# Spreading the first layer's edge-group sums over 27 of the 32 FFN steps of a tile

## The reference

```python
# layer 0, h = layernorm(x)
agg = segment_sum(h[src] * w1, dst)              # 256 features an edge
deg = segment_sum(ones, dst)
x = x + concat(agg / max(deg, 1), h) @ W.T + b
# experts of 512 hidden features, relu, top 2 of 8
x = x + sum_e combine_e * (relu(layernorm(x) @ W1_e + b1_e) @ W2_e + b2_e)
# layer 1: p = relu(layernorm(x) @ Wp.T + bp), 128 features an edge
x = x + p @ W1.T + b1 + sqrt(segment_sum(w * (p*p)[src], dst)) @ W2.T + b2
# experts of 256 hidden features, gelu, top 2 of 8
```

## Time and profile before

| what | us |
|---|---|
| median of the 3 runs | 3453.04 |
| the profiled execution | 3462.63 |
| its span, first to last instruction | 3460.8 |
| PE busy | 2546.9 (74%) |
| DVE busy | 1772.4 (51%) |
| ACT busy | 1138.6 (33%) |
| POOL busy | 1687.6 (49%) |
| mean granted TensorE clock | 0.87 of full speed |

### The profile page before, as it was taken

One profiled execution on the slowest core, in us unless ns is written; L12 is line 12 of the kernel. 1 busy time (PEld: TensorE's weight loads), 2 busy tenths in 40 slices (PEclk: granted clock), 3 DMA queues, 4 the chain that ended last, 5 costly groups with the idle time before them and its releaser, 6 DMA issues.

```text
span 3460.8 us, 47385 instructions
## 1 busy us (share of the span) xinstructions
PE 2546.9 (74%) x17983; PEld 1431.0 (41%) x17983; DVE 1772.4 (51%) x4296; ACT 1138.6 (33%) x1835; POOL 1687.6 (49%) x1678
## 2 busy tenths in 40 slices
PE   0147878878787887979798862357778777777897
PEld 0123434434343444434344652334444444444455
DVE  7463645445464545646465642334544444544565
ACT  3022423333232323324244550112332322333355
POOL 3646354352635345263532106666666666666620
PEclk9997989889898988989899985568888898878899
DMA  5523122221313222131311121212222212222110
GB/s 219 174 73 87 58 83 64 72 80 54 98 57 92 62 74 77 58 99 54 91 48 54 35 72 46 54 43 54 58 58 61 59 52 55 59 58 60 52 36 11
DMA packets 115790, 237.80 MB, mean 69 GB/s; under 512 B 30291, under 2 KB 69581, under 8 KB 115045
## 3 DMA queue, kind: packets, MB, share of 16 engines
q0 software_dynamic: 66560, 163.68, 17.0%
q1 hardware_dynamic: 48996, 71.05, 6.1%
HBM read 208.95 MB, written 25.67 MB: 68 GB/s over the span
## 4 chain that ended last, share of the span: by engine, by line
PE 45%; another core or an unknown queue 19%; DVE 15%; issue 13%; ACT 6%; DMA 1%; POOL 1%; DVEq 0%; ACTq 0%; SPq 0%; POOLq 0%
PE psY L697 16%; PE psH L667 15%; PE psM L761 3%; PE psE L657 3%; DVE hsc L1255 3%; PE psE L649 3%; DVE hid L1250 3%; ACT hid L1432 2%; PE psC L674 1%; DVE acc L1091 1%; ACT hsc L1439 1%; PE psM L713 1%; DVE mag L949 1%; ACT L1432 1%
## 5 line engine op out<-in xcount | busy, mean ns | idle before, releaser
L574 POOL DMA_INDIRECT ring<-table,src_s x1664 | 1659.4, 997 | 1575.6 <-PE psE L653 647.6
L697 PE MATMUL psY<-hsc,wbuf 128*128 128x512 f16 (+2 forms) x4032 | 974.6, 377 | 327.9 <-DVE acc L1091 127.5
L667 PE MATMUL psH<-xnT,wbuf 128*128 128x512 f16 (+2 forms) x4032 | 980.6, 381 | 64.3 <-issue 39.4
L1432 ACT ACTIVATE hid<-psH,b,scl 128x512 f32<-128x512 f32 (+2 forms) x672 | 485.8, 723 | 1553.8 <-PE psH L667 868.3
L697 PEld LDWEIGHTS psY<-hsc,wbuf 128*128 128x128 f16 x4032 | 375.6, 102 | 847.7 <-issue 221.9
L1250 DVE TENSOR_TENSOR hid<-hid,psC 128x512 f32<-128x512 f32 (+2 forms) x672 | 415.6, 618 | 557.3 <-ACT hid L1432 384.7
L667 PEld LDWEIGHTS psH<-xnT,wbuf 128*128 128x128 f16 x4032 | 390.4, 105 | 433.2 <-issue 155.9
L1091 DVE TENSOR_TENSOR acc<-acc,psE 128x120 f32 (+1 forms) x416 | 98.3, 236 | 881.4 <-remote 663.0
L1255 DVE TENSOR_TENSOR hsc<-hid,hsc 128x512 f16<-128x512 f32 (+2 forms) x672 | 415.8, 619 | 0.4 <-ACT hsc L1439 0.3
L1439 ACT ACTIVATE hsc<-hid 128x512 f16<-128x512 f32 (+2 forms) x672 | 379.8, 565 | 7.0 <-DVE hid L1250 6.7
L657 PEld LDWEIGHTS psE<-ohbuf,ring 128*128 128x128 f32 x1664 | 264.8, 233 | 52.0 <-DMA ring<-table,src_s 20.2
(11 more groups left out here) (154 smaller groups left out, 1730.4 us busy)
## 6 DMA issues: line engine op xcount, KB each, us to landing
ring<-table,src_s POOLq DMA_INDIRECT x1664
wbuf<-w_in SPq DMA_DIRECT2D x2, 4096.0 KB, 20.8
wbuf<-x_in SPq DMA_DIRECT2D x7, 896.0 KB, 11.5
table<-ring SPq DMA_DIRECT2D x7, 896.0 KB, 3.6
feat<-table SPq DMA_DIRECT2D x11, 512.0 KB
xin<-x_in SPq DMA_DIRECT2D x11, 512.0 KB
x_d<-x SPq DMA_DIRECT2D x11, 512.0 KB
xin<-x_d SPq DMA_DIRECT2D x11, 512.0 KB
```

The lines of the kernel that those rows point to most:

```text
L574: pool.indirect_dma_start(out=l.ring[:, g % l.R, k, :], out_offset=None, in_=l.table, in_offset=bass.IndirectOffsetOnAxis(ap=src_s[:, c:c ...
L667: last = mm(psH[n % 2][:, 0:TT[t]], l.w1(e, i, k, c), x[:, j, k, 0:TT[t]], start=(k == 0 and m == 0), stop=(k == KD - 1 and m == 2))
L697: last = mm(psY[d][:, 0:TT[t]], l.w2(e, i, c, d), hsc[n % 2][:, j, 0:TT[t]], start=False, stop=(n == l.M - 1 and m == 2))
L1432: f(hid[n % 4][:, 0:TT[t]], psH[n % 2][:, 0:TT[t]], (ACT.Relu, ACT.Gelu)[l.i], scale=l.un_up, bias=l.b1[:, n // l.HC, n % l.HC:n % l.HC + ...
```

## The change

Only the placement of groups changes what the engines do in the loop. `turn` of layer 0 goes from 28 to 18. `plan` gives each step a weight (`place`): the columns of its tile plus 64, and each of the four places before the FFN loop 1200 (`LEAD`). The groups of a tile are spread over steps 18 to 31 of tile t-2 and 0 to 12 of tile t-1 in proportion to that weight, with half a group of lead in layer 0 (`early`).

```diff
+LEAD = 1200
...
-                self.turn = (28, 1)[i]
+                self.turn = (18, 1)[i]
+                self.early = (0.5, 0.0)[i]
...
-                for t in range(1, NT):
-                    gs = list(sh.groups(t))
-                    early = len(gs) * (self.M - self.turn) // self.M
-                    late = gs[early:]
-                    for k, g in enumerate(gs[:early]):
-                        if t == 1:
-                            self.begun[k * 4 // early].append(g)
-                        else:
-                            n = self.turn + k * (self.M - self.turn) // early
-                            steps[self.M * (t - 2) + n].append(g)
-                    for k, g in enumerate(late):
-                        steps[self.M * (t - 1) + k * self.at_take // len(late)].append(g)
+                for t in range(1, self.NT):
+                    turns = self.place(t)
+                    gs = list(self.groups(t))
+                    whole = sum(w for w, _ in turns)
+                    k, passed = 0, turns[0][0]
+                    for i, g in enumerate(gs):
+                        while passed * len(gs) <= (i + self.early) * whole and k < len(turns) - 1:
+                            k += 1
+                            passed += turns[k][0]
+                        n = turns[k][1]
+                        (self.begun[n] if t == 1 and k < 4 else steps[n]).append(g)
                 self.steps = steps
 
+            def place(self, t):
+                def step(x):
+                    return self.TT[x] + 64
+                late = [(step(t - 1), self.M * (t - 1) + n) for n in range(self.at_take)]
+                if t == 1:
+                    return [(LEAD, k) for k in range(4)] + late
+                return [(step(t - 2), self.M * (t - 2) + n) for n in range(self.turn, self.M)] + late
```

More of the change, by code:

```diff
@@ L35, with __init__ @@
 XA = 4
+LEAD = 1200
 class Shape:
-    def __init__(self, n, e):
+    def __init__(self, n, e, layer):
         blocks = -(-n // P)
-        rest = blocks - 5
-        assert rest % SUB == 0 and blocks % XR == 0 and rest >= 4 * SUB
+        first, last = ENDS[layer]
+        full = blocks - sum(first) - sum(last)
+        assert full % SUB == 0 and blocks % XR == 0 and full >= 4 * SUB and last[-1] == 1
         self.n, self.e = n, e
-        self.B = [SUB] * (rest // SUB) + [2, 2, 1]
+        self.B = first + [SUB] * (full // SUB) + last
         self.NT = len(self.B)
@@ L787, in _ @@
                 general_sums(l)
-                for g in sh.groups(0):
+                for g in l.groups(0):
                     sum_first(l, [g])
@@ L806, in _ @@
                 up(l, 0, 1)
-                for t in range(NT):
-                    last = t == NT - 1
+                for t in range(l.NT):
+                    last = t == l.NT - 1
                     for n in range(l.M):
@@ L1102, in take @@
                     hold(dve)
[L1103 removed]
+                wait(dve, l.lin_summed, l.CB[u])
                 if l.i == 0:
@@ L1306, in _ @@
                     pass
+                for k in range(l.at_split[1], l.at_split[2]):
+                    matrix_low(l, k)
                 begin(1)
@@ L1309, in _ @@
                 normed_low(l, 0)
+                for k in range(l.at_split[2], 2 * NX):
+                    matrix_low(l, k)
                 begin(2)
@@ L1478, in _ @@
                 act.wait_ge(l.scales_ready, 1)
-                for k in range(2 * NX):
+                for k in range(l.at_split[0]):
                     matrix_high(l, k)
@@ L1588, in laid_out @@
         "partmask": partmask.reshape(9 * NX, 3),
-        "floor": np.tile(floor, (P, 1, 1)),
+        "floor": np.tile(floor, (P, 1, 1, 1)),
     }
```

289 lines of the change are left out of this document (153 added, 136 removed).

## The result

| | median us | runs | ratio to before |
|---|---|---|---|
| before | 3451.57 (3449.07 to 3456.6) | 4 | |
| after | 3248.73 (3241.68 to 3256.43) | 4 | 0.9411 (95%: 0.9386 to 0.9436) |

The change saves 202.8 us by the medians; the forecast was 202. Between the two profiled executions (spans of 3460.8 and 3244.1) it saves 216.7; that of before was above its median.

The account below looks back on a forecast made before the run. TensorE was taken to bound layer 0, interrupted by sums meeting POOL's gathers. Savings 156 + 14 + 29 + 11 − 8 = 202 us took the profiled 3462.6 to 3261, by the median 3251 us; range 3130 to 3390 for 8 times in 10.

Parts of the forecast that it names:

- What bounds the kernel: Layer 0: TensorE carries it but is interrupted; sums meeting a gather finish late, 38.7 us a tile in stalls and slow clock.
- The bare tile of 113.7 us: A layer 0 tile without stalls: first half 54.2 us plus second half 59.5, against 152.4 measured before.
- The halves with their stalls: Tiles 1 to 8: first half 63.5 us, second 69.4, together 132.9 instead of 152.4, saving 156 us.
- The 1.5 for DVE: Second half of tiles 1 to 8: added windows and one-hots fill DVE in steps 25 to 28, costing 1.5 us.
- Tiles 0 and 9: Tile 0 takes 137.4 us instead of 151.5, saving 14; tile 9 takes 120.9 instead of 150.5, saving 29.
- Tiles 10 to 12: Last layer 0 tiles: tile 10 saves 0, tile 11 8 us and tile 12 3, 11 together.
- Ahead of the loop: Before the first FFN loop: groups 23 to 25 need gathers first; loss of 8 us, between 1 and 15.
- Layer 1: One step of two sums moves and one more group is begun: 0, within 5 us either way.
- Cover: POOL's 47.94 us wait disappears, and no POOL wait in tiles 1 to 8 exceeds 15 us.
- The sums run unhindered when spread: Rival: sums wait only because 15 come close together; a tile takes 115.0 us, the kernel 3080 us; chance 0.14.
- The stalled second half: Rival: all nine second-half sums cost 2.6 us more; a tile takes 146.4 us, the kernel 3384 us; chance 0.16.
- the slower case: Rival: each of 17 sums meets a gather, 2.6 us each; a tile takes 157.9 us, the kernel 3501; chance 0.08.

Follow-up runs that it names:

- ones_weights: Kernel before, layer 0's sums taking a constant matrix as weights instead of the gathered rows, on a quiet chip: 2970.4 us against 2973.36.
- plain_copies: Kernel before, layer 0's indirect gathers replaced by plain transfers of the same bytes, on a quiet chip: 2832.7 us against 2973.4.
- start_pairs: Changed kernel with four groups of tile 1 ahead of tile 0's FFN loop instead of seven, on a quiet chip: 2849.04 us against 2976.70 before.
- ones_weights_2: Kernel before, layer 0's sums taking a constant matrix instead of gathered rows, on the chip with late sums: 3450.9 us against 3451.3.
- plain_copies_2: Kernel before, layer 0's indirect gathers replaced by plain transfers of the same bytes, on the other quiet chip: 2834.5 us against 2976.7.
- few_matmuls: Kernel before with 12 matmul pairs in a layer 0 sum instead of 28, low parts left out, on a quiet chip: 2993.2 us against 2976.7.

## Why the prediction was right, step by step

**What bounds the kernel.** Right for this chip, as far as it goes: sums that meet a gather are seen to end late, sums that find POOL idle take 0.99 us to their window. But it is not a matter of sums alone: hidden blocks and graph products are late with them, and part of the lateness comes after PE's work is done. One reading was wrong: of POOL's 1575.6 us of waiting in the earlier trace rows, 647.6 end with a sum, 41% and not most. One sentence was too strong: that "the rate of gathers is no bound by itself". It holds over a tile, but in steps 0 to 12 fifteen sums need eleven gathers beyond the ring's four, 55 us, and POOL stands idle while the ring is full. On the quiet chips that is the bound of the old plan (ones_weights: 5.0 us from sum to sum), and plain_copies shows it by taking it away: 126.4 to 113.8.

**The bare tile of 113.7 us.** Right: 113.5 measured in start_pairs, in halves of 53.8 (54.2 by the working) and 59.7 (59.5).

**The halves with their stalls.** The first half was forecast at 63.5 and measured at 63.1 on the mean over tiles 1 to 8 (from the first L714 matmul of step 0 to that of step 16); the second at 69.4 and 68.1. The totals of the stalls were near (8.0 + 1.3 against 63.1 − 53.8 = 9.3; 9.9 against 68.1 − 59.7 = 8.4), their parts were not, and so the totals are in part luck. What each step lost is seen beside start_pairs, which has the same steps on a quiet chip (a step from its first matmul of `down` to the next step's, mean of tiles 1 to 8; a pair with the steps behind it, up to the next sum). In the first half the three pairs cost 1.6, 0.3 and 0.8 us, 2.8 together where I gave 7.2; the sum of step 7 alone costs 5.0 and that of step 12 1.6, where I gave 0.8 to all the others. In the second half the pairs cost 0.5, 2.4 and 5.2, 8.1 together for 7.2. The sum of step 23, two steps after the last, has its window 1.9 us late (1030.06 to 1032.96 is 2.90), and PE loses nothing by it. So there is no price of 2.4 for a pair: what a late result costs depends on who waits for it. And DVE was not full. Steps 25 to 28 after, which I expected to be over 95% busy on DVE:

```profile
1035.30:1053.40 18.10, 13.89 (x135) 6.91 (x135) 12.74 (x37) 5.54 (x10) 11.54 (x12) 0.98 0.31 88
```

70%, and 5.2 us longer than the 12.90 of the same steps in start_pairs on a quiet chip. The 1.5 for DVE is in none of these rows by itself.

**Tiles 0 and 9.** 136.7 (forecast 137.4) and 122.1 (120.9).

**Tiles 10 to 12.** 21.0 us instead of 11: tile 10, put at nothing, gained 8.1. It had one sum in its second half and gets five in steps 19, 21, 24, 27 and 29, which are far enough apart to cost little more than their 0.70, while the four that leave its first half take their stalls with them.

**Ahead of the loop.** The one term outside its bounds: 16.6 us for a forecast of 8, with 15 as the upper end. I had counted gathers that had to be waited for, not sums that would meet them. The chip with late sums charges that here too (PE, POOL, DVE, and the transposes of the gates on PE):

```profile
247.77 0.96 PE L666 MATMUL psE<-ohbuf,ring 128*128 128x40 f16 x24
...
256.88 0.94 POOL L591 DMA_INDIRECT ring<-table,src_s  x1 [0.30 <-issue]
...
258.02 0.28 DVE L1110 TENSOR_TENSOR acc<-acc,psE 128x120 f32 x1 [7.99 <-remote]
...
263.60 0.64 PE L800 MATMUL psM<-ident_b,c 128*72 128x128 bf16 x4 [13.29 <-issue]
```

The window of group 22 comes 10.25 us after its sum, 0.20 after POOL's last issue, and DVE ranks the gates behind it. Without late sums the same start costs 4.5 to 7.3 us; with the 10.25 − 0.99 = 9.3 of this window that is 13.8 to 16.6, and 16.6 was measured. The match proves little: the window of group 21 is late as well (sum at 240.89, window at 247.39) and is in no term of this sum.

**Layer 1.** 3.3 us less in its loop and 3.9 more before it: within the 5 given.

**The total.** 202 was worked out from the profiled execution, and between the two profiled executions 216.7 were saved: 13.7 more than forecast in tiles 1 to 8, 10.0 more in tiles 10 to 12, 8.6 less ahead of the loop, and 0.4 less in the rest. Like for like the forecast was 14.7 us too small, and that the medians differ by just 202.8 is luck.

**Cover.** POOL's idle 47.94 us in the second half are gone, as said; its longest wait in tiles 1 to 8 is 16.6 us, not under 15.

**The rivals.** "The sums run unhindered when spread" is what the quiet chips do, with the mechanism that its text gave: 15 sums close together never catch up with their supply. It forecast a tile of 115.0; 113.5 was measured. The stalled second half and the slower case did not come.

**What stays open.** Why one chip has late sums and two have not, and what it is in a gather that holds back PE's results. It is not the weight loads from the ring (ones_weights_2). That the notice of a finished result comes late accounts for about 1.3 us of a lateness and may account for more; in the longest stalls PE's own rows thin out too (behind the sum of 1180.94 the matmuls of `up` are issued with gaps of up to 1.04 us that no wait explains), so slow work is not excluded for the rest. Whether it is POOL's work for the indirect form, the transfers in flight or another path was to be told by plain_copies_2 and few_matmuls, which met a quiet chip. That results are late because of the gather, and not merely beside it, rests on their times in the traces and on no run that took the gather away on that chip.

## What to carry to other kernels

When a producer fills a small ring, place its consumers evenly over all the time there is: a ring of four covers four uses, and work bunched behind it runs at the producer's pace while the producer stands idle elsewhere. (The quiet chips show this; on the chip with late sums pairs in every third step did as well.) Take the bare length of a stage from rows in which nothing was late; here it held to 0.2 us. A price for each lateness on top of it, taken from two rows, did not hold. When one result of an engine is seen late, look at who else waits for that engine at the same moment before blaming that one piece of work. And before a per-cent figure is carried further, run it on a second chip: the old plan's loss was 39 us a tile on one chip and 13 on another, and for different reasons.

## What the runs showed of the hardware that I had not expected

The same kernel took 3451 us on one chip and 2973 and 2977 on two others, with runs within 1% of each other on each. In layer 0 the gathers are issued as fast on each (0.94 to 0.95 us and 0.30 between); what differs is how long after its issue a sum is seen to end while POOL works. The same sum of step 2 of tile 5 has its window 3.95 us later in the profile of the result (944.90 to 948.85), and on a quiet chip, with POOL issuing all the while, 1.76 us later (start_pairs, PE and DVE):

```profile
816.18 0.76 PE L671 MATMUL psE<-ohbuf,ring 128*128 128x40 f16 x24
...
817.94 0.27 DVE L1115 TENSOR_TENSOR acc<-acc,psE 128x120 f32 x1
```

On the chip with late sums PE's results reach DVE and ACT in a bunch while POOL issues gathers: a window and the hidden block of the `up` behind it start 0.02 us apart (1026.46 and 1026.44) although 1.3 us of matmuls lie between them. In start_pairs no window and no hidden block has a wait of that kind.

On a quiet chip an indirect transfer of 128 rows costs POOL the same with 256 bytes a row as with 1024 (56.38 / 57 and 53.55 / 55 us busy, 0.99 and 0.97 each), and a plain one 0.53.
